# Last group's rows sent in stage one, expert weights 1 to 5 split beside them

## The reference

```
h = patches(x) @ W + b, in the order of a Hilbert curve   # 256 tokens of 192
h = concat(h, txt)                                        # 256 + 77 tokens per image
h = h + sdconv(layernorm(h))                              # 9 taps, softmax over the taps
x = layernorm(h)
scores, idx = top_k(x @ Wg, 2); weights = softmax(scores)
for k in 0, 1:                                            # capacity per expert: int(1.2 * N / 8)
    a = x[rows of expert e] @ W1[e]                       # 192 -> 1024
    y = (a[:, :512] * silu(a[:, 512:])) @ W2[e]           # 512 -> 192
    out[those rows] += weights[k] * y
h = h + out
```

## Time and profile before

| | us |
|---|---|
| median of 3 runs | 1472.23 |
| lowest, highest | 1465.93, 1474.36 |
| the profiled execution | 1466.77 |
| its span, first to last instruction | 1465.0 |
| TensorE busy in the span | 1208.3 (82%) |
| VectorE busy | 1018.7 (70%) |
| GpSimd busy | 685.6 (47%) |
| ScalarE busy | 464.6 (32%) |
| mean granted clock of TensorE | 0.906 of full |

### The profile page before, as it was taken

One profiled execution on the slowest core, in us unless ns is written; L12 is line 12 of the kernel. 1 busy time (PEld: TensorE's weight loads), 2 busy tenths in 40 slices (PEclk: granted clock), 3 DMA queues, 4 the chain that ended last, 5 costly groups with the idle time before them and its releaser, 6 DMA issues. The chain is left out here.

```text
span 1465.0 us, 30800 instructions
## 1 busy us (share of the span) xinstructions
PE 1208.3 (82%) x8700; PEld 1012.8 (69%) x8701; DVE 1018.7 (70%) x2367; ACT 464.6 (32%) x1197; POOL 685.6 (47%) x530
## 2 busy tenths in 40 slices
PE   6998988988989898841740278999999999999995
PEld 5776767776757676631430267988888898898895
DVE  4117959999999999996855367666666666666663
ACT  2011222323332132312031344444444444444442
POOL 1000221766666566755466324454554544455454
PEclk9998999998989899875765679999999999999998
DMA  9994553665656463629321524544444444444442
GB/s 321 398 322 127 140 164 90 174 172 159 176 164 170 115 179 96 162 76 268 103 60 51 132 33 52 66 59 61 65 57 62 59 60 61 58 65 57 62 60 28
DMA packets 215171, 175.31 MB, mean 120 GB/s; under 512 B 121864, under 2 KB 198694, under 8 KB 215104
## 3 DMA queue, kind: packets, MB, share of 16 engines
q1 hardware_dynamic: 170128, 115.36, 32.0%
q0 software_dynamic: 34720, 34.38, 14.5%
q10 hardware_dynamic: 10256, 24.73, 4.6%
HBM read 69.24 MB, written 88.47 MB: 108 GB/s over the span
## 5 line engine op out<-in xcount | busy, mean ns | idle before, releaser
L1233 POOL DMA_INDIRECT out<-yb,meta x182 | 297.6, 1635 | 339.6 <-DMA out<-yb,meta 200.8
L1017 PE MATMUL bankK<-normedT,conv_w 128*128 128x333 f32 x864 | 277.5, 470 | 0.0
L128 POOL DMA_INDIRECT expert_inputs<-slot_rows,slots x176 | 231.8, 1317 | 85.3 <-issue 59.9
L1306 DVE TENSOR_TENSOR hidden<-silu,bankU 128x256 f32<-128x256 f32 x364 | 153.1, 421 | 154.0 <-PE bankU L1346 98.5
L1262 ACT ACTIVATE silu<-bankG 128x256 f32<-128x256 f32 x364 | 139.2, 384 | 306.6 <-PE bankG L1346 306.6
L1017 PEld LDWEIGHTS bankK<-normedT,conv_w 128*128 128x128 f32 x864 | 169.1, 202 | 77.7 <-issue 12.2
L1359 PE MATMUL bankY<-expert_weights,hidden_high 128*128 x728 | 179.8, 247 | 0.8
L1360 PE MATMUL bankY<-expert_weights,hidden_high 128*128 x728 | 179.8, 247 | 0.0
L1361 PE MATMUL bankY<-expert_weights,hidden_low 128*128 x728 | 179.6, 247 | 0.0
L709 DVE TENSOR_TENSOR prod<-window_values,kb 128x960 f32<-128x960 f32 (+1 forms) x135 | 167.9, 1253 | 3.6
L727 DVE TENSOR_TENSOR hidden_group<-hidden_group,prod 128x960 f32<-128x960 f32 (+1 forms) x135 | 169.0, 1252 | 0.5
(11 more groups left out here) (162 smaller groups left out, 2304.2 us busy)
## 6 DMA issues: line engine op xcount, KB each, us to landing
patches<-in_x SPq DMA_DIRECT2D x16, 1536.0 KB, 8.6
expert_inputs<-prod ACTq DMA_DIRECT2D x6, 3430.0 KB, 23.5
token_rows<-rowbuf SPq DMA_DIRECT2D x32, 492.0 KB
window_values<-token_rows SPq DMA_DIRECT2D x32, 264.0 KB, 5.5
hidden_group<-token_rows SPq DMA_DIRECT2D x32, 264.0 KB, 7.0
window_values<-token_rows SPq DMA_DIRECT2D x32, 192.0 KB, 5.7
kb<-token_rows SPq DMA_DIRECT2D x32, 148.5 KB, 4.7
token_rows<-rowbuf SPq DMA_DIRECT2D x32, 148.0 KB
```

The lines of the kernel that those rows point to most:

```text
L128: nc.gpsimd.indirect_dma_start(out=xslots[:, :], out_offset=bass.IndirectOffsetOnAxis(ap=idx[g % 2][:, k, r:r + 1], axis=0), in_=xrow[g % ...
L1017: mm = T_.matmul(bankK[(u + t) % 2][:, 0:L], conv_w[:, t // 2, k, :], qT[u][:, t, k:k + L], start=(k == 0), stop=(k == K - 1))
L1233: nc.gpsimd.indirect_dma_start(out=out[:, :], out_offset=bass.IndirectOffsetOnAxis(ap=meta[t % NMETA][:, c, 0:1], axis=0), in_=yb[v][:, c, ...
L1306: V.tensor_tensor(hf[j % 2][:, :], sg[j % 2][:, :], bankU[j][:, 0:TS], ALU.mult)\
```

## The change

All 22 scatters of the last group are issued in stage one. Experts 1 to 5 are split in stage one as well, behind expert 0. The raw weights lie two slots further on instead of one (`raw_at(e + 2)`), so an upper half waits only for the lower half of the expert two before it. Experts 6 and 7 each get a staging buffer of their own and are split in tiles 3 and 5: the upper half at the head of that tile, the lower half at the end of the tile before it, now behind `evac_y`. TensorE's tiles 0 to 5 wait for all six early splits. In the slab of stage one the patches come first and the taps' products lie in slot 1, so that the loads of raw weights find their slots free.

```diff
+EARLY = 6
...
         def split_high(act, e, raw):
-            wait(act, w_low, e)
+            wait(act, w_low, e - 1)
...
+            xb = [in_slab(f"patches{u}", [128, 2, KC * TI]) for u in range(2)]
             wp_sb = in_slab("wp_sb", [128, KC, D])
...
-            xb = [in_slab(f"patches{u}", [128, 2, KC * TI]) for u in range(2)]
...
-            prodL = [w_all[:, E - 1, u, 0:2 * SLICES[0][1] * D].bitcast(fp32) for u in range(2)]
+            prodL = [w_all[:, 1, u, 0:2 * SLICES[0][1] * D].bitcast(fp32) for u in range(2)]
...
                 for e in range(1, E - 2):
-                    load_w(sp, e, raw_at(e + 1), w_loaded[1])
+                    load_w(sp, e, raw_at(e + 2), w_loaded[1])
...
-                for r in range(R):
-                    scatter_rows(NG - 1, r, last_sent)
+                for n in range(TOPK * R):
+                    scatter_rows(NG - 1, n, last_sent)
...
                 split_high(act, 0, raw0)
+                act.wait_ge(w_loaded[1], 64 * (E - 3))
+                for e in range(1, EARLY):
+                    split_high(act, e, raw_at(e + 2))
...
                 split_low(dve, 0, raw0)
+                for e in range(1, EARLY):
+                    split_low(dve, e, raw_at(e + 2))
...
-            wstage = sb("wstage", [128, WROW])
+            wstage = [sb(f"wstage{n}", [128, WROW]) for n in range(2)]
...
+            SPLIT_AT = {3: E - 2, 5: E - 1}
...
             def raw_of(e):
-                return wstage[:, :] if e == E - 1 else raw_at(e + 1)
+                return wstage[e - E + 2][:, :] if e >= E - 2 else raw_at(e + 2)
...
-                for n in range(R, TOPK * R):
-                    scatter_rows(NG - 1, n, last_sent)
...
-                act.wait_ge(w_loaded[1], 64 * (E - 3))
-                for e in range(1, AHEAD):
-                    split_high(act, e, raw_of(e))
...
-                        if first_body(i) and t + AHEAD < E:
-                            if t + AHEAD == E - 2:
-                                act.wait_ge(w_loaded[2], 128)
-                            split_high(act, t + AHEAD, raw_of(t + AHEAD))
+                        if first_body(i) and t in SPLIT_AT:
+                            act.wait_ge(w_loaded[2], 128)
+                            split_high(act, SPLIT_AT[t], raw_of(SPLIT_AT[t]))
...
-                for e in range(1, AHEAD):
-                    split_low(dve, e, raw_of(e))
...
-                        if first_body(i) and t + AHEAD < E:
-                            split_low(dve, t + AHEAD, raw_of(t + AHEAD))
                         if t or not first_body(i):
                             evac_y(i, t - 1)
+                        if first_body(i) and t + 1 in SPLIT_AT:
+                            split_low(dve, SPLIT_AT[t + 1], raw_of(SPLIT_AT[t + 1]))
...
                     if first_body(i):
-                        pe.wait_ge(w_low, t + 1)
+                        pe.wait_ge(w_low, max(EARLY, t + 1))
```

More of the change, by code:

```diff
@@ L1170, in build @@
             block = st.enter_context(nc.Block())
-            AHEAD = 2
             w_flat = w_all[:, :, :, :].rearrange("p e s f -> p (e s f)")
```

## The result

The changed kernel takes 1461.59 us in the median of eight runs, the kernel before 1471.5 in eight runs beside them: a ratio of 0.9943, with an interval of 0.9924 to 0.9962. It is faster by 0.57%, just over what such a measurement can tell from no change. The medians are 9.9 us apart, and the forecast's sum was -9.9. That the two agree to a tenth is luck: the interval reaches from 5.6 to 11.2 us, and when both kernels were run again on another occasion the medians were 7.2 us apart.

A forecast was written before the change was run, and what follows sets the result against it. TensorE bounds the steady expert stage; the gain lies before and inside the first tiles. +14.3 - 25.6 + 1.4 = -9.9 us gives 1456.9 from the profile or 1462.3 from the median; named 1460, range 1447 to 1470.

The forecast's parts named there:

- Scatters beside the splits: Last group's scatters in stage one: one gets through per VectorE split, numbers 4 to 9; the last ends at 822.7.
- GpSimd against VectorE: Stage one, by the skill's rule: further splits start some 0.85 us late, 4.3 us over five; sum -5.6 instead of -9.9.
- Change of stage: From GpSimd's last end in stage one to the first instruction behind it: 4.6 us.
- What is late next: Head of the expert stage: eight weight loads hold up the transposing load; first matmul at 840.8, 14.3 us later.
- S: Start of stage two, the expert stage: forecast at 827.3 instead of 804.2, bounds 816.8 and 833.7.
- The stores' row: Profile row of the hidden group's stores: 112.5 KB land in 2.0 us alone, 9.5 (median) behind weight loads.
- Tiles 0 to 8: Expert stage: 50.7 us instead of 76.3, so 25.6 come back; the two splits left cost 1.4 together.
- The sum: Whole kernel: +14.3 to the first matmul, -25.6 in the tiles, +1.4 for two late splits, giving -9.9 us.
- transposing loads that pass the weights: Rival, head of expert stage: weights do not delay these loads; first matmul S + 8.9, sum -14.5, 1455 us; chance 0.13.
- no contention: Rival, stage one: VectorE costs GpSimd nothing; stage change 10.5 us earlier, sum -20.4, time 1450; chance 0.07.
- starved scatters: Rival, stage one: no scatter gets in between splits; 6.4 us later, sum -3.5, time 1466; chance 0.05.
- dear splits: Rival, tiles 3 and 5: splits cost 4.6 us each as before, 9.2 for 1.4; sum -2.1, time 1468; chance 0.10.

The follow-up runs named there:

- the one-input run: Changed kernel with lower halves of experts 1 to 5 in stage one computed from one tensor, not two; 22 scatters took 34.7 us, no ratio given.
- the splits-only kernel: Changed kernel with the second eleven scatters back in the expert stage, the splits staying in stage one; 0.9859 of the kernel before.
- the run with another queue: Changed kernel with the weight loads of experts 6 and 7 issued by ScalarE on its own queue, at the same time; 0.9931 of the kernel before.
- the run with one per tile: Changed kernel with only experts 0 and 1 split in stage one, 2 to 7 in tiles 1 to 6; 1.0004 of the kernel before.

## Why the prediction was right

The forecast was 1460 (1447 to 1470) and -9.9 us. Measured are 1461.6 and -9.9 between medians, -10.2 in the stretch of the first pair of profiles. The second time they are -7.2 between medians, and -7.5 in the stretch of the second pair of profiles. So the direction and the size were right, and the agreement to a tenth is luck. Counted from F, as the forecast was (8.2 us earlier than the times above), the last scatter ended at 822.3 for 822.7, the transposing load landed at 841.3 for 840.5 and the first matmul came at 841.7 for 840.8. Step by step:

- **Scatters beside the splits.** Forecast: one per split, numbers 4 to 9 held up, 38.6 us from first start to last end. Measured: 38.2, exactly these six. Right, and not only by coincidence of the sum: with one, two, four or five splits in stage one, one, two, four or five scatters are held up. Which ones, and whether the first takes 2.70 or 3.77, depends on where the first split falls between two scatters; the four profiles with six whole splits and all 22 scatters in stage one have 38.2 to 39.6. Two inputs are not needed for it, as the one-input run shows.
- **GpSimd against VectorE.** By the rule of the Trainium skill (SBUF — State Buffer, the section on the two separate sides) a scatter that runs would block VectorE too, and each further split would start 0.85 us late. The trace does not agree: six splits start 3.0 us apart, no more than their own length, with a scatter between each two.
- **Change of stage.** Forecast 4.6 us from GpSimd's last end, measured 5.5 (830.51 to 835.98). This term was 0.9 too small. All eight profiles with 22 scatters in stage one have 5.5; all five with eleven in the expert stage have 4.6 (820.23 to 824.81 in the splits-only kernel). Why is open.
- **What is late next.** Forecast S + 13.5 for the first matmul, measured S + 13.9. That is the least of six profiles: with the loads first in the stage and 22 scatters ahead, the others have S + 14.6 to S + 15.6. So the wait for the weights was foreseen and its size came out somewhat small. The reason was named too narrowly. The step "in the same queue" says that the load waits because it stands behind the weights in SyncE's queue. In the changed kernel this fits: the last weights land by 848.7, the load at 849.5. But the run with another queue showed that the load is as late there, while it shares the engines with the weights; of the two remedies, only moving the loads in time worked. The stores' row on which I chose cannot tell the two apart: from 687 to 693 us SyncE's queue took 84.0% of the engines' time and GpSimd's 21.4%, so the engines were full.
- **Tiles 0 to 8.** Forecast 50.7 and 1.4 for the two splits, measured 50.9 in all. So the tiles came out 1.2 better than the 52.1 of the forecast. Each split costs next to nothing, as TensorE has a tile's work in hand; the run with one per tile shows where that ends (8.9 us a tile), and the ones in tiles 1 and 7 where the cover is missing.
- **The sum.** First matmul +15.2 (forecast +14.3), tiles -25.4 (forecast -24.2). The two errors are 0.9 and 1.2 us and nearly cancel. In the second profile they do not: +17.2 and -24.7 against the second profile of the kernel before, -7.5 in all.
- **The scale.** I named 1460 between 1456.9 and 1462.3 as the profile of before lay 5.5 us below its median. The median was the right one to add to (1471.5 in eight runs).

Of the rivals, transposing loads that pass the weights fall by the landing of 7.92 us (and another queue did not let them pass), no contention and starved scatters are ruled out by the six rows of 2.70, and dear splits by the tiles.

What the forecast did not say is that the change's two halves have opposite signs: splits alone are worth 17.5 us of stretch, scatters alone cost 8.6. Its first term, +14.3, has the loss in it, but I never asked what the splits would give without the scatters. The version with the second eleven scatters left in place beats both kernels, by 1.4% and 0.8% (0.9859 against the 0.9940 of the changed kernel beside it).

## What to carry to other kernels

When a wait is removed at the head of a stage, look at what was hidden behind it: here 2.88 MB of weights, which then stood in front of the first 0.2 MB load on which everything waits. Extra work on an engine beside the bound one is cheap if it comes at a distance that lets that engine catch up; here two tiles apart cost next to nothing, and one tile closer the same work costs 2.5 us each time (8.9 less 6.34). Before moving a load to another queue, count its packets and those that it will share the engines with. And test the halves of a change alone, since a gain in the sum can hide a loss.

## What was not expected of the hardware

- The first transposing load took 3.0 to 3.6 us where the weight loads were out of the way, 5.2 where they came later in the same stage, 7.9 to 9.6 behind 2.88 MB of them in its own queue, and 11.15 beside them in another queue. There the two queues moved 964 packets each in 9.65 us, 0.20 MB and 1.77 MB.
- A VectorE instruction with one SBUF input (2816 elements in 1.63 us) held a scatter up to 0.84 us behind its own end, as one with two inputs does (0.85); a reduction of 1188 elements in 1.39 us did not.
- A scatter that was held up let the next VectorE instruction start at once: six splits of 3.09 us at a spacing of 3.0.
- With 11 scatters of the last group ahead of it the change of stage took 4.6 us from GpSimd's last end, with 22 it took 5.5, in 13 profiles without exception. Why is open.
